# One written order of steps for each engine over all eight batches, in place of a loop over turns

## The chip, the cores and the metric

One core of a Trainium2 chip runs the kernel. The metric is device time in microseconds (us) from one launch. The engines named are PE (TensorE), DVE (VectorE), ACT (ScalarE), POOL (GpSimd) and SP (SyncE, which here only issues DMAs). Each engine takes its own instructions strictly in order, and engines meet at semaphores.

## The reference

Input x is 8 batches of 256 tokens by 128 features. Each batch passes four blocks, each closed by a residual sum and a LayerNorm:

```
x = layernorm(x + attention(x))   # 16 heads, a standard and a "geometric" softmax, both causal, mixed by a gate
x = layernorm(x + ffn(x))         # 128 -> 352 -> 128, activations and weights rounded to FP4 in blocks of 16
x = layernorm(x + mamba(x))       # 256 channels, 16 states, recurrence hc = a*hc + b over 256 tokens
x = layernorm(x + lora_ffn(x))    # 128 -> 512 -> 128, with a correction made from tokens 1 to 16
```

No batch depends on another.

## The kernel before

Every part of the work is a Python generator. A `yield` ends a step, and a step is a wait or two with the few instructions behind it. The parts, with the letters that the changed kernel uses for them:

- `prep` (p): transposes x, makes q, k, v and the line vectors, and splits them in three bf16 parts, which SP stores to DRAM and loads back as the attention's operands (L574, L588).
- `core` (c): 24 blocks of scores on PE with the row maximum on DVE (L1056). Then, with the maxima in the operands, 24 blocks again on PE, exponentials on ACT (L861) and the products with v on PE. ACT copies each half's sum out (att, L866).
- `norm_std` (N) and `norm` (n): divide by the softmax sums on DVE (L1078 to L1080: cstd, then cgeo), mix and project on PE, add the input (z, L1093), LayerNorm statistics (L974, L977), root on POOL (L732, L733), normalise on DVE (L985). N is one step; n has three on DVE: cgeo, z with its statistics, and the normalising that gives x1.
- `ffn` (f): 12 steps on DVE. The first five quantize x1 (L956 to L969), the rest is the gated product (L1110), its quantizing, z (L1101), and x2.
- `mamba` (m): hx (L1128), gate and convolution on PE, dbc (L1133), delta and u (L1137, L1141).
- `scan` (s), with `products` (u) on POOL (L769) and `rows` (r) on SP (L618): 16 DVE scans (L1152), each pair followed by the product with C (L1161, and L1157 for the last pair, half by half). PE sums the products in ps_y (9 steps). ACT makes the decay factors (L924), 16 steps.
- `mamba_out` (o): y (L1167), the projection into ps_n on PE, z (L1101) with statistics, x3.
- `lora_ffn` (l): the last block; y_out and its store.
- `warm` (w): matmuls of zeros into ps_y (two a step) which only keep PE active. There are 203 such steps in all with those of `warm_fill` and `warm_late`.
- `setup` (x): weights.

The kernel is pipelined over batches in **turns**. Turn k holds norm, ffn, mamba and scan of batch k, core and norm_std of batch k+1, prep of k+2, mamba_out and lora_ffn of k-1. `PLAN` gives, for each engine and part, a planned time for each step, and `interleave` issues the steps of a turn in the order of these times. All of a turn's steps are issued before any of the next. Turns -2 to 0 and 5 to 8 are written out; turns 1 to 4 are one body in a hardware loop, whose waits compare with register values. `EDGE` holds other times for turns -1, 0, 7 and 8.

```python
            for k in range(-2, 1):
                turn(k)
            with eng.Fori(1, BATCH - 3) as k:
                turn(k)
            for k in range(BATCH - 3, BATCH + 1):
                turn(k)
```

At the end of a steady turn the order on DVE is 25 steps s, then N. The next turn begins o n c c n o c c n o f f f f f. On PE the end is c s s s s N s, then n c p c n p n p c p c o. Written in letters, both repeat in each turn from 1 to 6 (turn 6 without the p).

Of the kernel before, what the change touches and what calls it, by code (L numbers as in the profile page):

```python
# [39 lines left out]
PLAN = {  # L40
    "sp": {
        "lora_ffn": [26.4, 57.5],
        "prep": [45.8, 57.7, 61.4, 63.8, 97.9, 101.2],
        "core": [48.9, 55.2, 55.3, 73.9, 76],
        "rows": [68.7, 71.2, 71.5, 71.8, 72.1, 82.9, 87.2, 90.1, 93.8],
    },
    "pool": {
        "core": [-2, 43],
        "prep": [15.5, 28.9, 40.6, 43.9],
        "lora_ffn": [31.2, 41.9],  # L50
        "mamba": [68.9],
        "products": [71.1, 72.4, 74.1, 75.4, 77, 78.3, 80.1, 81.4, 83.7, 85, 93.5, 94.8, 96.5, 97.8, 99.4, 99.6],
        "norm": [14.6],
        "ffn": [42.1, 42.2],
        "mamba_out": [15.8],
    },
    "act": {
        "prep": [10.4, 12.8, 14.9, 16.4, 17.9, 19.1, 22.9, 35, 42.3],
        "core": [0.3, 68.9, 69.5, 70, 70.5, 71, 72.6, 72.7, 77.4, 78.6, 79.2, 81.5, 82.6, 84.4, 84.9, 85.5, 85.6,
                 86.8, 87.4, 87.9, 90.5, 93.2, 93.3, 93.4, 93.8, 94.7, 96.6],  # L60
        "norm": [12.1],
        "lora_ffn": [21.7, 31.6],
        "ffn": [22.7, 28.8, 41.1],
        "mamba": [47.1, 47.2, 47.3, 47.6, 63.8, 65.3],
        "scan": [67.4, 69, 71.4, 75.5, 78, 79.3, 81.7, 82.9, 85.7, 86.5, 89, 92.4, 94.8, 94.9, 97.3, 98.5],
    },
    "dve": {
        "mamba_out": [2.8, 8.8, 13.9],
        "norm": [4.6, 7.8, 11.5],
        "core": [5.5, 6.1, 9, 9.6, 20.4, 21, 22.5, 24.3, 25.8, 34.1, 34.7, 36.7, 40.5, 45.6, 46.2, 47.4, 53.8, 55.5,  # L70
                 56.2, 56.9, 57.5, 58.7, 59.3, 59.9, 60.6, 62.6],
        "ffn": [15.8, 17.4, 17.8, 18.4, 19.4, 26, 28.8, 29.7, 30.8, 32.6, 38.5, 40.7],
        "prep": [22, 24.8],
        "lora_ffn": [23.9, 25.5, 36.2, 42.8],
        "mamba": [46, 55.1, 60.9, 77.7],
        "scan": [77.8, 77.9, 78, 78.1, 78.2, 78.3, 78.4, 78.5, 78.6, 78.7, 79.8, 81.1, 82.3, 83.5, 84.7, 87.7, 87.8,
                 92.1, 93.3, 94.5, 97.3, 98.7, 99.3, 99.9, 101.2],
        "norm_std": [110.4],
    },
    "pe": {  # L80
        "norm": [0, 2.4, 3.7],
        "prep": [0.9, 2.8, 3.9, 5, 6.6, 8.4, 24.1],
        "core": [0.8, 1.9, 4.1, 5.1, 7.3, 7.7, 17.7, 20.3, 21.5, 24.7, 25.2, 32, 35.5, 35.6, 37, 43, 49.7, 50.1, 51,
                 52.8, 53.4, 54.7, 55, 55.9, 56.6, 57.9, 58, 58.6, 60.1, 60.7, 61.6, 62, 63.3, 64.1, 64.4, 64.9,
                 65.5, 66, 66.7, 69.7, 70.4, 73.8, 74.2, 74.5, 75.1, 77.3, 77.7, 78, 78.7, 80.8, 81.2, 81.5, 82.4,
                 84.6, 84.9, 85.3, 85.6, 86.9],
        "mamba_out": [6],
        "lora_ffn": [13.5, 15.9, 21.6, 24, 26.1, 28],
        "ffn": [16.6, 19.2, 22.5, 22.6, 30.4, 32.8],
        "mamba": [42.2, 45, 45.1, 46, 50.8, 51.9, 52.1],  # L90
        "scan": [68, 71.6, 75.6, 86.2, 89.7, 97.5, 102.5, 105.9, 106.4],
        "norm_std": [106.1],
        "warm": [7.2, 7.6, 8.3, 13.1, 14.5, 21.1, 22.7, 38.3, 38.4, 39.5, 40.5, 41.5, 41.9, 42, 42.1, 42.5, 53.5,
                 57.8, 59.5, 61.5, 77.8],
    },
# [1495 lines left out]
```

## Time and profile before

| | us |
|---|---|
| median of 3 runs | 845.85 (844.6 to 849.32) |
| profiled execution, first to last instruction | 846.4 |
| PE busy | 706.0 (83%) |
| DVE busy | 610.1 (72%) |
| ACT busy | 409.4 (48%) |
| POOL busy | 396.6 (47%) |
| turns 1 to 6, from one y (L1167) to the next | 90.3 to 91.7 each |

The profile has no time of its own for the profiled execution besides its span; the span lies 0.55 us above the median of the runs, inside their spread. PE's busy time includes the matmuls of zeros.

### The profile page before, as it was taken

To read this page: it belongs to the slowest core of one execution; us is meant where nothing else is said; L and a number is where in the kernel's file an instruction comes from. 1 tells how busy PE (TensorE), PEld (TensorE's weight loads), DVE (VectorE), ACT (ScalarE), POOL (GpSimd) and SP (SyncE) were. 2 spreads that over 40 slices of the span, in tenths; PEclk is the share of its full clock that TensorE was granted. 3 is DMA by queue.
4 is the path that set the end of the run, shared out by engine and by line. 5 is a ranking of instruction groups with operands and counts; after the bars stand their busy time and mean duration, and the time that the engine had idled before them with its cause. 6 is when DMAs were issued, how large, how long until landed. Compare 5 with 4: busy or idle time off the path is not lost. (4 is left out here: it accounts for less than half of the span.)

```text
span 846.4 us, 12934 instructions
## 1 busy us (share of the span) xinstructions
PE 706.0 (83%) x4422; PEld 418.4 (49%) x4422; DVE 610.1 (72%) x1083; ACT 409.4 (48%) x832; POOL 396.6 (47%) x475
## 2 busy tenths in 40 slices
PE   5378768898889889997989888988898799876678
PEld 2244435445644565455645564456554564444235
DVE  1763475887869786969598677978697859744692
ACT  1225332763568254845385446815582438432532
POOL 6641322572449323952476344923393028411561
PEclk7679968999999999999999999999999999968898
DMA  5321200440035104420144013500442014000410
GB/s 132 85 97 61 98 25 21 153 160 9 26 129 168 51 0 133 130 107 0 53 166 147 5 39 127 173 27 1 152 131 85 1 34 158 26 0 7 146 55 7
DMA packets 41221, 66.12 MB, mean 78 GB/s; under 512 B 8041, under 2 KB 30398, under 8 KB 38846
## 3 DMA queue, kind: packets, MB, share of 16 engines
q1 hardware_dynamic: 39006, 64.58, 23.3%
q10 hardware_dynamic: 2176, 1.05, 0.4%
q8 instruction: 22, 0.36, 0.2%
q14 instruction: 17, 0.14, 0.1%
HBM read 57.68 MB, written 7.86 MB: 77 GB/s over the span
## 5 line engine op out<-in xcount | busy, mean ns | idle before, releaser
L769 POOL TENSOR_TENSOR shared<-u,bcrow 128x512 f32<-128x512 f32 x128 | 207.9, 1658 | 103.1 <-DVE u L1141 69.4
L1056 DVE TENSOR_REDUCE mx<-ps_s 128x2 f32<-128x512 f32 (+1 forms) x192 | 126.9, 685 | 68.3 <-PE ps_s L1195 66.4
L1195 PE MATMUL ps_s<-stack_mem 72*128 72x128 bf16 (+3 forms) x1024 | 138.9, 252 | 28.8 <-DVE mx L1056 16.8
L1152 DVE TENSOR_TENSOR_SCAN shared<-ps_f,shared 128x512 f32<-128x512 f32 x128 | 150.9, 1210 | 15.9 <-PE ps_y L1195 9.0
L1195 PE MATMUL ps_y<-shared,ident 128*128 128x512 f32 (+1 forms) x288 | 124.3, 566 | 12.3 <-DVE shared L1161 10.9
L924 ACT ACTIVATE ps_f<-delta,amat 128x255 f32<-128x255 f32 x256 | 110.2, 475 | 36.7 <-DVE shared L1152 22.6
L1195 PEld LDWEIGHTS ps_s<-stack_mem 74*128 74x128 bf16 (+1 forms) x1024 | 80.8, 100 | 90.3 <-DVE mx L1056 32.1
L1195 PE MATMUL ps_y<-zero_bf 128*128 128x512 bf16 x419 | 118.6, 396 | 1.2 <-DVE zero_bf L997 1.1
L861 ACT ACTIVATE probs<-ps_s 128x512 f32<-128x512 f32 x192 | 104.4, 596 | 20.0 <-PE ps_s L1195 20.0
L732 POOL TENSOR_TENSOR rstd<-mv,cst 128x2 f32<-128x2 f32 x32 | 6.2, 195 | 174.5 <-DVE mv L977 174.5
L1195 PEld LDWEIGHTS ps_y<-shared,ident 128*128 128x128 f32 x288 | 51.5, 193 | 58.7 <-issue 34.3
L1161 DVE TENSOR_TENSOR shared<-shared,bcrow 128x1024 f32<-128x1024 f32 x56 | 76.3, 1363 | 1.9
L1195 PE MATMUL ps_s<-causal,ident_bf 128*128 128x256 bf16 (+1 forms) x192 | 62.3, 326 | 4.1 <-DVE mx L1056 2.8
L1195 PEld LDWEIGHTS ps_y<-zero_bf 128*128 128x128 bf16 x419 | 41.8, 102 | 37.0 <-issue 12.9
L1195 PE MATMUL ps_s<-causalT,ident_bf 128*128 128x256 bf16 (+1 forms) x192 | 59.8, 312 | 0.2
L1195 PE MATMUL ps_v<-probs,vz 128*32 128x256 f32 (+1 forms) x1024 | 54.9, 332 | 4.1 <-ACT probs L861 3.8
L1195 PEld LDWEIGHTS ps_v<-probs,vz 128*32 128x32 f32 x1024 | 26.7, 109 | 41.4 <-ACT probs L861 20.5
L1195 PE MATMUL ps_n<-lmem 1*128 1x128 f32 (+1 forms) x224 | 32.3, 293 | 11.3 <-ACT lmem L935 6.5
L1195 PEld LDWEIGHTS ps_n<-lmem 1*128 1x128 f32 (+1 forms) x224 | 28.1, 198 | 20.2 <-ACT lmem L935 9.3
L715 POOL TENSOR_TENSOR vals<-vals,parts 128x1024 f32<-128x1024 f32 x8 | 17.7, 2216 | 39.8 <-ACT parts L844 39.8
L1195 PE MATMUL ps_f<-wguT,xqT_mem 128*128 128x352 f32 x64 | 33.0, 649 | 0.5 <-ACT xqT_mem L877 0.5
L790 ACT ACT_TABLE_LOAD x25 | 32.1, 1283 | 1.3 <-PEq L1576 0.8
(213 smaller groups left out, 1060.0 us busy)
## 6 DMA issues: line engine op xcount, KB each, us to landing
bcrow<-bc_dram SPq DMA_DIRECT2D x64, 512.0 KB, 4.2
stack_mem<-stack_dram SPq DMA_DIRECT2D x96, 192.0 KB
stack_dram<-parts SPq DMA_DIRECT2D x24, 256.0 KB, 2.3
x_tm<-in_L_attn_x_dram ACTq DMA_DIRECT2D x8, 128.0 KB, 2.1
xb<-in_L_attn_x_dram SPq DMA_DIRECT2D x8, 128.0 KB, 2.2
out_dram<-y_out SPq DMA_DIRECT2D x8, 128.0 KB, 2.0
fmem<-in_L_attn_conv_w_dram SPq DMA_DIRECT2D x1, 512.0 KB
...
```

The lines of the kernel that those rows point to most:

```text
L715: G.tensor_tensor(rest1[:], vals[:], parts[:, 0], ALU.subtract).then_inc(rest1_sb, 1)
L732: chain(G.tensor_tensor(dst, v, eps.to_broadcast([P, TT]), ALU.add))
L769: G.tensor_tensor(bx[:, j % 2, c], u[:, c].unsqueeze(1).to_broadcast([P, 2, T]), bcrow[:, j % RING, 0], ALU.mult).then_inc(bx_sb, 1)
L790: nc.scalar.preload_act_table_set("natural_log_exp_and_others")
L861: A(probs[:, g % 3, (n % 3) * 512:(n % 3 + 1) * 512], ps_s[:, n % 3], ACT.Exp).then_inc(p_exp, 1)
L924: last = A(adisc[:, c, n, 1:T], delta[:, c, 1:T], ACT.Exp, scale=amat[:, c, 2 * j + n:2 * j + n + 1])
L1056: V.tensor_reduce(mx[:, a, min(i, 1), hd[0]:hd[-1] + 1:2], ps_s[:, n % 2].rearrange("p (h n) -> p h n", h=len(hd)), AX.X, ALU.max).then_in ...
L1152: V.tensor_tensor_scan(hs[:, j % HB, c].rearrange("p n t -> p (n t)"), ps_f[:, c, :], bx[:, j % 2, c].rearrange("p n t -> p (n t)"), 0.0, ...
L1161: V.tensor_tensor(hs[:, j % HB], hs[:, j % HB], bcrow[:, j % RING, 1].unsqueeze(1).to_broadcast([P, NC, 2, T]), ALU.mult).then_inc(hc_dve, 1)
L1195: return nc.tensor.matmul(o, lhsT, rhs, start=start, stop=stop, **kw)
```

## The change

The tables `PLAN`, `EDGE` and `SPLIT`, the function `interleave`, the hardware loop and the clearing of the chain semaphores at each turn go. Each engine gets one string of letters for the whole run. Every letter issues the next step of its part, and a part goes to its next batch when its generator is through:

```diff
+class Stream:
+    def __init__(self, steps, batches=range(BATCH)):
+        self.steps, self.batches, self.now = steps, iter(batches), None
+
+    def step(self):
+        if self.now is None:
+            self.now = self.steps(next(self.batches))
+            next(self.now)
+        if next(self.now, DONE) is DONE:
+            self.now = None
...
+        def run(name, **streams):
+
+            streams = {letter: Stream(*s) if isinstance(s, tuple) else Stream(s) for letter, s in streams.items()}
+            for letter in "".join(ORDER[name].split()):
+                streams[letter].step()
...
             def ffn(b):
 
                 yield
+                if not is_first(b):
+                    dve.wait_ge(conv_ps, b * 2)
                 yield from quantize(flat(xq[:]), flat(x1[:]), T // BLK, T, xq_sb, xqT, flat(xq[:]))
...
+            def warm(_):
+                yield
+                if scanned[0] and not summing[0]:
+                    pe.wait_ge(yg_sb, scanned[0])
+                zero_step()
```

The number of steps of each letter is the same on every engine, the 203 warm steps among them. Only their order differs, and it now differs from turn to turn. From the strings, each turn's entry on DVE, beginning with N (s are the last scan steps of the batch before; before the change, all of them stood ahead of N):

```
turn 1:  N n o n c c o n f o c c f f f f
turn 2:  N s s s s n o n c c o n c c f o f f f f
turn 3:  N s s n o n o n f c c o f c f f f
turn 4:  N s n s s s s n o c c o n f f c o c f f f
turn 5:  N s l n s s n o n o f o c c f c c f f f
turn 6:  N s n s s n s s n f o f f f f
turn 7:  N s s s n s s n o n o f o f f f f
```

In turn 0, n n c c n f c f c f f f stands for c c c n c n n f f f f f. On PE, the first n of turns 2 to 7 stands ahead of the last one to three s, and in turns 4 to 6 its second and third too. From the entry of m on, DVE has m and 7 or 8 c, m and 5 or 6 c, then m m (before: m c c c m, 8 c, m c m). On PE c steps stand between the convolution steps of m (m c m c c m m c c m c c m c c m; before m w c m m m c c m c m m). Between PE's last m and last s stand 11, 11, 12, 8, 17 and 9 w in turns 1 to 6, where it was 5, and 34 c where it was 39 (31 in turn 4). Between the last f and the first m PE has 6, 1, 4, 3, 1 and 4 w where it was 8. On SP, in turns 4 and 5, the three stores of the parts (L574) stand behind the last r, not ahead of the first, and from turn 1 on one or both of the stack loads of `prep` (L588, six DMAs each) pass into the next turn, the second behind the load of x3's rows (l).

## Rows read from the trace of the kernel before

**Rows 1.** Windows by turn: length, busy PE PEld DVE ACT POOL, clock, DMA share, GB/s.

```profile
281.70:372.50 90.80, 80.80 (x541) 48.67 (x540) 72.59 (x131) 50.53 (x103) 47.80 (x56) 0.98 0.26 86
...
462.90:554.60 91.70, 82.06 (x540) 49.88 (x539) 72.67 (x131) 50.54 (x103) 47.79 (x56) 0.96 0.26 86
554.60:645.40 90.80, 80.92 (x541) 48.92 (x542) 72.62 (x132) 50.59 (x103) 47.79 (x56) 0.98 0.26 86
645.40:735.70 90.30, 78.86 (x519) 47.10 (x520) 71.94 (x126) 44.23 (x90) 33.81 (x30) 0.96 0.15 51
```

**Rows 2.** DVE in order of time, from turn 1 into 2: start, us, instruction, [idle before].

```profile
279.56 0.69 DVE L1157 TENSOR_TENSOR shared<-shared,bcrow 128x512 f32<-128x512 f32 x1
...
281.67 0.69 DVE L1167 TENSOR_TENSOR y<-ps_y,gsilu 128x512 f32<-128x512 f32 x1 [0.26 <-PE ps_y L1195]
...
282.89 0.42 DVE L1080 TENSOR_TENSOR cgeo<-ps_n,rec 128x256 f32<-128x256 f32 x1
283.23 1.28 DVE L1056 TENSOR_REDUCE mx<-ps_s 128x4 f32<-128x512 f32 x2
285.75 0.42 DVE L1093 TENSOR_TENSOR z<-ps_n,xb 128x256 f32<-128x256 f32 x1 [1.24 <-PE ps_n L1195]
...
286.73 0.25 DVE L977 BATCH_NORM_AGGREGATE mv<-bn 128x2 f32<-128x6 f32 x2
289.98 0.42 DVE L1101 TENSOR_TENSOR z<-ps_n,x2b 128x256 f32<-128x256 f32 x1 [3.01 <-issue]
...
292.54 0.60 DVE L985 TENSOR_SCALAR x<-z,mv,rstd 128x128 f32<-128x128 f32 x2
...
294.05 0.41 DVE L956 TENSOR_REDUCE qamax<-x 128x16 f32<-128x256 f32 x1
```

**Rows 3.** PE in order of time at the same place.

```profile
281.47 0.66 PE L1199 MATMUL ps_n<-ident,att 128*128 128x128 f32 x4
...
288.78 1.11 PE L1195 MATMUL ps_n<-moutw,y 128*128 128x128 f32 x8
```

**Rows 4.** ACT at the same place: the copy of the second half of attention.

```profile
273.75 0.60 ACT L866 ACTIVATE att<-ps_v 128x512 f32<-128x512 f32 x1 [0.44 <-PE ps_v L1195]
```

**Rows 5.** POOL at the same place: the second instruction of the root.

```profile
287.33 0.70 POOL L733 TENSOR_TENSOR rstd<-rstd,cst 128x2 f32<-128x2 f32 x1
```

**Rows 6.** DVE in turn 2, mamba and scan.

```profile
328.86 0.69 DVE L1056 TENSOR_REDUCE mx<-ps_s 128x4 f32<-128x512 f32 x1 [5.62 <-PE ps_s L1195]
...
330.56 0.47 DVE L1133 TENSOR_SCALAR dbc<-ps_f,dbcb 48x256 f32<-48x256 f32 x1
...
332.80 3.98 DVE L1056 TENSOR_REDUCE mx<-ps_s 128x4 f32<-128x512 f32 x6 [0.57 <-PE ps_s L1195]
336.70 0.42 DVE L1137 SCALAR_TENSOR_TENSOR delta<-fmem 128x256 f32<-128x256 f32 x1
...
339.73 1.22 DVE L1152 TENSOR_TENSOR_SCAN shared<-ps_f,shared 128x512 f32<-128x512 f32 x1
...
363.81 2.34 DVE L1152 TENSOR_TENSOR_SCAN shared<-ps_f,shared 128x512 f32<-128x512 f32 x2 [1.48 <-PE ps_y L1195]
```

**Rows 7.** Window from PE's last mamba step to its last scan step, turn 2.

```profile
332.20:372.30 40.10, 37.18 (x291) 19.11 (x290) 37.01 (x41) 29.45 (x69) 29.42 (x25) 1.00 0.47 164
```

**Rows 8.** The same window, matmuls of zeros alone (PE, PEld, DVE).

```profile
332.20:372.30 40.10, 2.96 (x10) 0.97 (x10) 0.00 (x0) 1.00 0.47 164
```

**Rows 9.** SP in order of time: the stack loads of turn 2.

```profile
355.87 10.22 SPq L588 DMA_DIRECT2D stack_mem<-stack_dram  x12
```

**Rows 10.** Instructions of the loop's line, by queue: ns min/median/max.

```profile
L524 PEldq COMPARE_BRANCH  x4: 76/210/239, 280.4 to 553.5; - x4
```

**Rows 11.** Turn 0: ACT's copy of attention.

```profile
90.28 0.60 ACT L866 ACTIVATE att<-ps_v 128x512 f32<-128x512 f32 x1 [0.98 <-PE ps_v L1195]
```

**Rows 12.** Turn 0: DVE's cgeo.

```profile
96.51 0.42 DVE L1080 TENSOR_TENSOR cgeo<-ps_n,rec 128x256 f32<-128x256 f32 x1
```

**Rows 13.** A window of the FFN's first matmuls in turn 2.

```profile
298.40:301.80 3.40, 3.40 (x11) 1.97 (x12) 2.37 (x5) 2.41 (x5) 0.00 (x0) 0.51 0.00 0
```

More of the change, by code:

```diff
@@ L37 @@
 LN_SHIFT = 20
[L40 to L95, printed above, removed]
-}
@@ L770, in products @@
                                         bcrow[:, j % RING, 0], ALU.mult).then_inc(bx_sb, 1)
-            def scan(b):
-                for j in POOL_HC:
-                    yield
-                    pool.wait_ge(hs_sb, b * 16 + 2 * j + 2)
-                    G.tensor_tensor(hs[:, j % HB], hs[:, j % HB], bcrow[:, j % RING, 1].unsqueeze(1).to_broadcast(S4),
-                                    ALU.mult).then_inc(hc_pool, 1)
-            run(pool, chain, "pool", ((prep, 2), (core, 1), (mamba, 0), (norm, 0), (ffn, 0), (products, 0), (scan, 0), (mamba_out, -1), (lora_ffn, -1)), setup)
+            run("pool", x=(setup, (0,)), p=prep, c=core, m=mamba, n=norm, f=ffn, u=products, o=mamba_out, l=lora_ffn)
         @block.scalar
@@ L937, in lora_ffn @@
                 exp_ln_tables()
-            run(act, chain, "act", ((prep, 2), (core, 1), (norm, 0), (ffn, 0), (mamba, 0), (scan, 0), (lora_ffn, -1)), setup)
+            run("act", x=(setup, (0,)), p=prep, c=core, n=norm, f=ffn, m=mamba, s=scan, l=lora_ffn)
         @block.vector
@@ L1186, in lora_ffn @@
                 (yield from layer_norm(2, b + 1, y_out, (y_stored, b * 16 + 16), b + 2)).then_inc(y_sb, 1)
-            run(dve, chain, "dve", ((prep, 2), (core, 1), (norm_std, 1), (norm, 0), (ffn, 0), (mamba, 0), (scan, 0),
-                                    (mamba_out, -1), (lora_ffn, -1)), setup)
+            run("dve", x=(setup, (0,)), p=prep, c=core, N=norm_std, n=norm, f=ffn, m=mamba, s=scan, o=mamba_out, l=lora_ffn)
         @block.tensor
@@ L1457, in mamba, with scan @@
                     mm(ps_f[:, c, 0:T], dupw[:, c * P:(c + 1) * P], dbc[:]).then_inc(dl_ps, 1)
[L1459 to L1461 removed]
+            def scan(b):
+                for j in range(N // 2):
                     halves = range(NC) if j == N // 2 - 1 else range(1)
@@ L1554, in lora_ffn @@
                 last.then_inc(f1_ps, 1)
-            run(pe, None, "pe", ((prep, 2), (core, 1), (norm_std, 1), (norm, 0), (ffn, 0), (mamba, 0), (scan, 0), (scan_late, -1), (warm, 0), (warm_fill, 1), (warm_late, -1),
-                                 (mamba_out, -1), (lora_ffn, -1)), setup)
+            run("pe", x=(setup, (0,)), p=prep, c=core, N=norm_std, n=norm, f=ffn, m=mamba, s=scan, w=(warm, range(10 ** 4)), o=mamba_out, l=lora_ffn)
 _INS = ['L0_attn_x', 'L0_attn_qkv_w', 'L0_attn_qkv_b', 'L0_attn_w1_write', 'L0_attn_w2_write', 'L0_attn_w1_read',
```

262 lines of the change are left out of this document (54 added, 208 removed), and 6 rows, old and new, of the table EDGE.

## The prediction

> **What bounds the kernel now.** I read the windows by turn first. Turns 1 to 6 take 90.3 to 91.7 us each. DVE works 72.6 us of turn 2 and PE 80.8, so no engine fills the turn [rows 1], and 11.3 of PE's 80.8 are matmuls of zeros (42 in that window). Then DVE in order of time, from one turn into the next [rows 2]. Here the reader is to see a chain with other work in its way. The last scan product ends at 279.56 + 0.69 = 280.25, and the quantizing of x1, with which the next batch's ffn begins, starts at 294.05: 13.8 us. In between are N, y, cgeo, two row maxima, z with statistics, a wait of 3.01 us for mamba_out's product, its z, two more maxima, x1 and x3. Attention's second half, all that x1 needs from outside, was copied out at 273.75 + 0.60 = 274.35 [rows 4], 5.9 us before the scan's end. It waited because every s stood ahead of n in the written order. So the period is the chain x1, ffn, mamba, scan, x1: 13.8 us of entry, then 45.7 from 294.05 to 339.7 and 31.4 of scan, 90.9 in all. The scan is DVE's own work but for one wait of 1.48 us for ps_y [rows 6]. Last the windows of PE: from its last mamba step to its last scan step it works 37.2 of 40.1 us [rows 7]. Ahead of that it has slack, inside it nearly none.
>
> **The change part by part.** Nothing is added to the arithmetic. I cost the order, by segments.
>
> Entry of the FFN. Prices [rows 2]: cgeo 1.03 (282.28 to 283.31), and N the same; from cgeo's end to its z 285.75 - 283.31 = 2.44 (PE mixes, ACT copies, PE projects); z with statistics 286.98 - 285.75 = 1.23, mamba_out's too; from statistics to a usable root about 1.1, since POOL is through at 288.03 [rows 5]; a pair of maxima 1.28; x1 and x3 0.60 each; y 0.69, not before 281.67 (1.4 after the scan's end); mamba_out on PE 1.11 plus about 0.3 to reach DVE [rows 3]. Laid end to end in the new order, counted from the scan's end, with what now stands inside the scan added:
> - Turn 1: cgeo to 3.0 (PE can turn att only behind its last scan step; in before it did so at 281.47 [rows 3]), y 3.7, z 5.4 to 6.7, maxima 8.0, mamba_out's z 8.1 to 9.3, x1 9.9. Saved 3.9. Moved in between the first two steps of quantizing: x3 and two maxima, 1.9. Net 2.0.
> - Turn 2: N in the scan (1.0); cgeo 1.0, y 2.1, z 4.0 to 5.2, maxima 6.5, mamba_out's z 7.8, x1 8.4, maxima 9.7. Saved 3.1, x3 inside costs 0.6. Net 2.5.
> - Turn 3: without the maxima 9.6. Saved 4.2; x3 and three maxima inside, 2.5. Net 1.7.
> - Turn 4: N and cgeo in the scan (2.1); z at once, maxima and y over PE's wait; x1 5.7. Saved 6.0, inside 1.9. Net 4.1.
> - Turn 5: cgeo before the last pair, whose 1.9 us cover most of the 2.44; x1 and mamba_out's z by 5.6. Saved 6.1, inside 3.2. Net 2.9. y_out's 0.6 is also put into this scan, but leaves the way of hx.
> - Turn 6: cgeo and z (3.3 with N, some 0.5 of wait) in the scan, x1 at once. Saved 9.4, y inside 0.7. Net 8.7.
> - Turn 7: as turn 5 (7.7). No core runs there, so I estimate the old entry at 13.8 less two pairs of maxima, 11.2. Saved 3.5, x3 inside 0.6. Net 2.9.
> Sum 24.8.
>
> Turn 0: att is there at 90.88 [rows 11], cgeo began at 95.90 and its main instruction at 96.51 [rows 12], behind maxima and PE's steps of prep. In the new order both n follow at once: 4.5 earlier, less two maxima inside the quantizing (1.3), and I take 3.5.
>
> What moved out of the entry (a pair of maxima, mamba_out's z, x3) needs cover. The waits of 5.62 and 0.57 between hx and delta [rows 6] are it, because PE now issues c between the convolutions. Price: two c on PE ahead of them, 1.2 us. Gain: between dbc and delta, six steps c instead of eight, of the 336.70 - 330.56 = 6.1 us between them, so 1.3 for two maxima, and mparts no longer between the deltas, some 0.5. I take 1.8. Net 0.6 a turn, 3.6 over six. If the cover is gone, 3 us a turn come back on the chain.
>
> Scan. PE's sums s2 and s3 now stand behind c49 to c53, not c44 and c56, so the 1.48 us wait should go: up to 9 us over six turns. But PE adds three n steps (2.2) and 3 to 12 w steps. At 2.96 us for 10 matmuls of which two are one step [rows 8], a step is 0.59 alone and 0.43 in a row, so six more on average are 2.8, and five c fewer save 2.6. That is 37.2 + 2.4 = 39.6 of 40.1 us: PE is full. Bounds 0 and 9; I take 0, since the row of PE's window is the nearer one. ACT has three exponentials ahead of the first decay factor and 6 to 9 ahead of the third; it works 29.5 of that window's 40.1 us, and I cost it at nothing beyond the 0.8 already in the 1.8.
>
> SP. In turns 4 and 5 the stack loads start some 4 us later than 355.87, behind the parts' stores, and the six of the first half take half of 10.22 us [rows 9], so they land near 366 where PE wants them at 372.8 or earlier by the gain: hidden. The second half now waits behind x3's rows, to about 14 us into the turn, and is wanted after 33: hidden. If the first weren't, PE's c, and y behind it, would be late by the excess. The wait on conv_ps in ffn is for a convolution of the batch before, 60 us old: nothing. The 203 w steps stay.
>
> Loop. Its branch takes 0.21 us on PE, four times [rows 10]. Turn 2 in the loop and turn 5 written out both take 90.80, turn 4 in the loop 91.70 [rows 1]: removing the loop is worth 0 to 1.5 us; I take 0. The Trainium skill (Runtime: NRT & Kernel Launch, Instruction fetch mechanics) says that a taken branch whose target lies outside the fetched window stalls for a DMA, and speaks for writing loops out. By it alone the change would gain something at each of four jumps; the equal turns say that this kernel hides it.
>
> Sum: 24.8 + 3.5 + 3.6 = 31.9. Seven entries are seven different orders, and with in-order engines each step that stands a little too early is paid in full, so I take three quarters: 23.9. **846.4 - 23.9 = 822.5 us.** The profiled span stands for the run; the median is 0.55 lower, which I leave in the range.
>
> **The rivals.**
> - The whole sum comes through and the ps_y waits go too, at two thirds of their 9: 846.4 - 31.9 - 6, about 808. For it: the longest waits of rows 2 and 6 all go. Against it: rows 7.
> - PE becomes the bound: the fills inside the scan window delay the sums, y follows PE, and only the slack ahead of m counts. The window then grows by the 2.4 us of work in six turns, 14 of the 24 are gone: about 837.
> - Slower: a wait on attention in front of the scan's sums. PE now has n ahead of s6 to s8, and DVE has cgeo ahead of the last scans. Att came 5.9 us before the scan's end; if it comes later than 3 us before that end, every further us holds both engines. It cancels the gain of 31.9 / 6 = 5.3 a turn when att slips by 2.9 + 5.3 = 8.2 us. ACT's new order, decay factors later, exponentials earlier, speaks against a slip. At 10 us slip, 6 x 1.8 above even: about 857.
> - The change does nothing: turns are held by something I don't see, and only the loop counts: 845 to 846.
> - The clock. One stretch in turn 2 ran at 0.51 of full, 1.2 GHz, in the FFN's first matmuls [rows 13], just behind a stretch in which PE waited for the quantizing. Fewer fills stand before m now. If each turn got one more such stretch on the chain, at half of 3.4 us, 7 x 1.7 = 12 us would be lost: 834. The Trainium skill (TensorE: Matmul & The Clock Gate, HAM oscillation) tells that waits of this kind bring the clock down; this row agrees.
>
> **How the numbers follow.** Chances: my forecast 0.55 (own range 812 to 832), whole sum 0.13, PE bound 0.12, clock 0.06, slower 0.07, nothing 0.07. A measurement here can tell 0.5%, that is 4.2 us. Faster by more (under 841.6): 0.86; within: 0.07; slower: 0.07. The range goes down to 803, which takes in the first rival, and up to 840, which takes in PE and clock and leaves out the last two.
>
> **What would show it.** In the profile after: y to y about 86 to 88 in turns 1 to 5 and the shortest into turn 6; from the last scan product to the quantizing 8 to 10 us in turns 1 to 3, about 5 in turns 4 and 5, under 2 in turn 6; the 3.0 us wait at mamba_out's z gone or under 1.5; cgeo between scans from turn 4 on; mx waits between hx and dbc down from 5.6; PE busy nearly as before in a shorter span. Wrong if cgeo waits for attention inside the scan, if DVE's wait for ps_y grows, if PE waits for the stack loads, or if the old waits show up again between f and m in equal size.

## The result and the profile after

| | before | after |
|---|---|---|
| median | 846.11 us (844.6 to 849.32) | 826.16 us (824.2 to 830.62) |
| ratio after / before | | 0.976, 95% interval 0.9725 to 0.9797 |
| profiled execution: time, span, granted clock | no time of its own, 846.4 span, 0.929 | 825.88, 824.1 span, 0.915 |

The change takes 20 us off, at a lower granted clock. Medians here and below are over all executions, while ratios leave out those over 1.5% above the same kernel's fastest (two of six in e6, one of six in e12). The page of the changed kernel, its first lines:

```profile
span 824.1 us, 12171 instructions
## 1 busy us (share of the span) xinstructions
PE 712.8 (86%) x4422; PEld 423.6 (51%) x4422; DVE 619.5 (75%) x1083; ACT 409.3 (50%) x832; POOL 394.3 (48%) x475
```

Windows from y to y, turns 1 to 6, columns as in [rows 1]:

```profile
185.50:272.20 86.70, 78.03 (x534) 47.76 (x535) 74.75 (x132) 50.35 (x103) 47.55 (x56) 1.00 0.31 105
272.20:365.40 93.20, 84.79 (x540) 51.46 (x540) 75.44 (x132) 51.06 (x103) 45.68 (x56) 0.93 0.21 73
365.40:459.80 94.40, 87.30 (x557) 53.85 (x557) 78.47 (x137) 51.12 (x106) 47.57 (x57) 0.91 0.27 86
459.80:546.10 86.30, 78.18 (x543) 48.19 (x542) 74.96 (x131) 50.54 (x103) 48.23 (x56) 1.00 0.28 90
546.10:633.50 87.40, 80.71 (x542) 49.30 (x540) 77.82 (x137) 49.81 (x102) 48.38 (x58) 0.98 0.29 89
633.50:720.00 86.50, 79.42 (x513) 47.77 (x513) 70.33 (x120) 44.23 (x90) 32.37 (x28) 0.92 0.20 67
```

Four turns lost 3.4 to 5.4 us against the 90.3 to 91.7 of before. Turns 2 and 3 got longer, and theirs is the clock that fell, to 0.93 and 0.91. Turn 6, which was to be the shortest, runs at 0.92 too.

DVE from turn 5 into turn 6, the place that answers to [rows 2]:

```profile
622.47 0.33 DVE L887 RECIPROCAL rec<-ps_n 128x32 f32<-128x32 f32 x1
...
625.75 0.42 DVE L889 TENSOR_TENSOR cgeo<-ps_n,rec 128x256 f32<-128x256 f32 x1
626.09 1.21 DVE L963 TENSOR_TENSOR_SCAN shared<-ps_f,shared 128x512 f32<-128x512 f32 x1
...
628.61 0.42 DVE L902 TENSOR_TENSOR z<-ps_n,xb 128x256 f32<-128x256 f32 x1 [0.58 <-PE ps_n L1005]
...
631.13 0.69 DVE L968 TENSOR_TENSOR shared<-shared,bcrow 128x512 f32<-128x512 f32 x1
631.74 0.60 DVE L794 TENSOR_SCALAR x<-z,mv,rstd 128x128 f32<-128x128 f32 x2
632.37 0.42 DVE L765 TENSOR_REDUCE qamax<-x 128x16 f32<-128x256 f32 x1
...
633.53 0.69 DVE L978 TENSOR_TENSOR y<-ps_y,gsilu 128x512 f32<-128x512 f32 x1
```

N, cgeo and z stand between the scan steps, x1 follows the last product (L968) at once, and y comes inside the quantizing: 0.5 us from scan end to qamax, against 11.6 into turn 6 before (13.8 into turn 2, [rows 2]). Into turn 3 it took 7.9 us:

```profile
363.32 0.81 DVE L968 TENSOR_TENSOR shared<-shared,bcrow 128x512 f32<-128x512 f32 x1
...
367.51 0.42 DVE L902 TENSOR_TENSOR z<-ps_n,xb 128x256 f32<-128x256 f32 x1 [1.47 <-PE ps_n L1005]
...
370.11 0.42 DVE L910 TENSOR_TENSOR z<-ps_n,x2b 128x256 f32<-128x256 f32 x1 [1.37 <-issue]
...
372.02 0.42 DVE L765 TENSOR_REDUCE qamax<-x 128x16 f32<-128x256 f32 x1
...
374.98 1.93 DVE L794 TENSOR_SCALAR x<-z,mv,rstd 128x128 f32<-128x128 f32 x2
```

The wait of 3.01 us at mamba_out's z [rows 2] is 1.37. But x3's normalising, moved into the quantizing, takes 1.93 us for its two instructions, where [rows 2] has 0.60.

**Where the time went.** The chain cut at its milestones on DVE, from the two traces (us; turns 1 to 7 summed):

| segment | before | after | difference |
|---|---|---|---|
| up to batch 0's qamax of x1 | 103.1 | 108.1 | +5.0 |
| from there to batch 0's scan end | 87.0 | 74.6 | -12.4 |
| entries: scan end to qamax of x1 | 92.1 | 43.3 | -48.8 |
| qamax to quantized x1 | 22.6 | 41.7 | +19.1 |
| quantized x1 to gated hidden (hff) | 56.2 | 62.6 | +6.4 |
| hff to z of the FFN | 81.6 | 81.5 | -0.1 |
| z to first scan | 162.4 | 159.5 | -2.9 |
| scan, with what was put in | 217.9 | 229.8 | +11.9 |
| last scan end to the end | 23.5 | 23.0 | -0.5 |

Each segment runs from the start of one instruction to the start of the next one named, scan end apart. qamax is the first instruction of the quantizing of x1, hff the gated product. Together -22.3, which is 824.1 - 846.4. (For z to first scan the two middle parts, to hx and on, are added.)

### The profile page after: what moved, and what is told of

Its sections match the earlier page's. It is cut to its first block and busy times, and to the rows that moved or that the text cites. A ratio compares the mean times of both kernels' runs of the same rounds, so it can differ in the third digit from the quotient of the medians.

```text
span 824.1 us, 12171 instructions
## 1 busy us (share of the span) xinstructions
PE 712.8 (86%) x4422; PEld 423.6 (51%) x4422; DVE 619.5 (75%) x1083; ACT 409.3 (50%) x832; POOL 394.3 (48%) x475
## 5 line engine op out<-in xcount | busy, mean ns | idle before, releaser
L586 POOL TENSOR_TENSOR shared<-u,bcrow 128x512 f32<-128x512 f32 x128 | 203.6, 1620 | 64.1 <-DMA bcrow<-bc_dram 34.3
L963 DVE TENSOR_TENSOR_SCAN shared<-ps_f,shared 128x512 f32<-128x512 f32 x128 | 151.1, 1208 | 11.8 <-ACT ps_f L733 7.1
L1005 PE MATMUL ps_s<-stack_mem 72*128 72x128 bf16 (+3 forms) x1024 | 143.7, 260 | 7.7 <-DVE mx L865 5.6
L1005 PE MATMUL ps_y<-shared,ident 128*128 128x512 f32 (+1 forms) x288 | 121.8, 553 | 8.8 <-DVE shared L972 8.0
L1005 PEld LDWEIGHTS ps_s<-stack_mem 74*128 74x128 bf16 (+1 forms) x1024 | 83.8, 102 | 63.0 <-DVE mx L865 19.4
L972 DVE TENSOR_TENSOR shared<-shared,bcrow 128x1024 f32<-128x1024 f32 x56 | 78.9, 1409 | 1.8
L1005 PE MATMUL ps_s<-causalT,ident_bf 128*128 128x256 bf16 (+1 forms) x192 | 61.5, 323 | 2.1 <-DVE mparts L872 2.1
L1005 PE MATMUL ps_v<-probs,vz 128*32 128x256 f32 (+1 forms) x1024 | 56.2, 338 | 1.8 <-ACT probs L670 1.4
L1005 PEld LDWEIGHTS ps_v<-probs,vz 128*32 128x32 f32 x1024 | 27.1, 110 | 33.4 <-ACT probs L670 13.8
L1005 PE MATMUL ps_n<-lmem 1*128 1x128 f32 (+1 forms) x224 | 37.7, 326 | 5.5 <-ACT lmem L744 3.0
L1005 PEld LDWEIGHTS ps_n<-lmem 1*128 1x128 f32 (+1 forms) x224 | 33.3, 228 | 14.9 <-ACT lmem L744 5.3
L1005 PE MATMUL ps_f<-wguT,xqT_mem 128*128 128x352 f32 x64 | 30.5, 611 | 3.9 <-ACT xqT_mem L686 2.4
```

The costliest lines, as they stand in the source:

```text
L586: G.tensor_tensor(bx[:, j % 2, c], u[:, c].unsqueeze(1).to_broadcast([P, 2, T]), bcrow[:, j % RING, 0], ALU.mult).then_inc(bx_sb, 1)
L963: V.tensor_tensor_scan(hs[:, j % HB, c].rearrange("p n t -> p (n t)"), ps_f[:, c, :], bx[:, j % 2, c].rearrange("p n t -> p (n t)"), 0.0, ...
L972: V.tensor_tensor(hs[:, j % HB], hs[:, j % HB], bcrow[:, j % RING, 1].unsqueeze(1).to_broadcast([P, NC, 2, T]), ALU.mult).then_inc(hc_dve, 1)
L1005: return nc.tensor.matmul(o, lhsT, rhs, start=start, stop=stop, **kw)
```

## The experiments

Steps are written with letter, batch and number: s1.24 is step 24 of batch 1's scan, w a step of zeros. All kernels are the changed one with another order, and compute the same; e3, e6, e7, e8, e9 and those built on them also have another number of steps of zeros. A minus in a diff is the changed kernel's order where nothing else is said. The changed kernel itself had 826.16, ratio 0.976.

**e1_old_order.** The former order on every engine, written out without the loop.

```diff
-    "dve": "ppxpxxxxxxxxcccc..."      # the new order
+    "dve": the letters of the former turns -2 to 8, one turn after another
```

> The old kernel's order of steps, turn by turn, written out as one string per engine in the new code: no hardware loop, no register values in the waits, no clearing of semaphores. If the loop is worth nothing (my costing, 0 to 1.5 us), 845 to 846 us and turns of 90.3 to 91.7 us. If the loop itself cost time (fetch stalls at the jumps), turns 1 to 4 get shorter and turns 5 and 6 don't, and the time falls towards 826.

Measured: 845.46 median (841.16 to 853.26), ratio 1.001 (0.9963 to 1.0054). The loop and its branch are worth nothing here, to within the 4 us of the interval; the 20 us are in the order.

**e2_setup.** One DVE step of batch 1's preparation, which waits 10.65 us in the middle of the weights' set-up, behind it.

```diff
- dve: x0.0 p1.0 x0.1 ... x0.8 c0.0 c0.1
+ dve: x0.0 x0.1 ... x0.8 c0.0 p1.0 c0.1
```

> The changed kernel with one DVE step moved: the first prep step of batch 1 (line squares' sums) goes behind the nine setup steps and the first maximum, where it was in the old order. In the changed kernel DVE waits 10.65 us at that step for POOL, in the midst of quantizing the weights, and the first row maximum starts at 56.2 us, not 50.6. If that in-order wait is what made the start late: first maximum near 51, time 820 to 822. Rival: the start is late from PE's low clock in the first core (27.3 us at 1.2 GHz from 57.7), and the moved step gives back under 1 us.

Measured: 827.76 (826.97 to 832.93), ratio 0.9799 (0.9723 to 0.9876); the first maximum at 56.9. The wait only moved: DVE was done sooner, and then waited 9.28 us for ACT's copy of the weights. ACT and PE had their own steps still in the new places; e6, which puts them back on every engine, has the first maximum at 49.7. So the late start is not this one step's.

**e3_fills_core0.** Nine steps of zeros more on PE inside batch 0's core, where the former order had them.

```diff
- pe: c0.2 c0.3 ... c0.10 c0.11 ... c0.56 c0.57
+ pe: c0.2 w c0.3 ... c0.10 w c0.11 ... c0.56 w c0.57
```

> The changed kernel with nine more steps of matmuls of zeros in the first batch's core on PE, behind the same core steps as in the old kernel. From the first row maximum to the copy of attention's second half it took 39.7 us before (clock 0.97) and 43.4 in the changed kernel (27.3 us at 1.2 GHz). If missing fills brought the clock down there: 40 us and clock near 1.0 in that stretch, time 821 to 823, all else being equal. Rival: the clock is low for the waits on DVE's setup just ahead; then the stretch stays at 43 and the time at 826 or a little above.

Measured: 827.88 (826.59 to 831.56), ratio 0.9794 (0.972 to 0.9868). From first maximum to last att copy it takes 43.6 us with them and 43.4 without, although the granted clock there rose from 0.69 to 0.77. That is the rival: the fills were not what batch 0 lacked.

**e5_entry_undone.** On DVE and PE every step n of batches 1 to 7 back behind the last scan step of the batch before; all else new.

```diff
- dve: s5.19 N6.0 s5.20 n6.0 s5.21 s5.22 n6.1 s5.23 s5.24 n6.2 f6.0 o5.0
+ dve: s5.19 N6.0 s5.20 s5.21 s5.22 s5.23 s5.24 n6.0 n6.1 n6.2 f6.0 o5.0
- pe: s5.5 n6.0 w w w n6.1 w n6.2 s5.6 s5.7 w s5.8 c7.0
+ pe: s5.5 w w w w s5.6 s5.7 w s5.8 n6.0 n6.1 n6.2 c7.0
```

> The changed kernel with the passing of the turn boundary by norm undone: on DVE and PE every n of batches 1 to 7 stands behind the last scan step of the batch before; all other steps keep their order. By the entries measured in the changed kernel (with cgeo and z taken out of the scan and laid behind it): turn 4 about +3, turn 5 +2, turn 6 +4, turn 7 +2, so 834 to 838 us. If passing the boundary is the whole gain, 846. If it is worth nothing because PE bounds the scan, 826.

Measured: 846.27 (840.95 to 852.45), ratio 1.001 (0.997 to 1.0052). That is the 846 named for "the whole gain", not the 834 to 838 worked out from the entries. DVE into turn 6, from the profiled execution, which at 852.45 was the slowest of ten:

```profile
647.82 0.69 DVE L968 TENSOR_TENSOR shared<-shared,bcrow 128x512 f32<-128x512 f32 x1
650.72 0.36 DVE L887 RECIPROCAL rec<-ps_n 128x32 f32<-128x32 f32 x1 [2.21 <-PE ps_n L1009]
...
654.20 0.42 DVE L902 TENSOR_TENSOR z<-ps_n,xb 128x256 f32<-128x256 f32 x1 [2.44 <-PE ps_n L1005]
...
656.58 0.60 DVE L794 TENSOR_SCALAR x<-z,mv,rstd 128x128 f32<-128x128 f32 x2 [1.16 <-POOL rstd L552]
```

8.7 us of entry with three waits, which the former order filled with maxima and y, and y is 9.9 us late here. Without the passing of the boundary nothing of the change's gain is left. But this isn't the former kernel again. Its entries add up to 71.1 us, still 21 less than before, and the 19.1 us more between qamax and quantized x1 eat most of that. Against the changed kernel the entries are 27.8 longer and the scans 7.6 shorter: the passing is worth 20 us net in this order. It doesn't follow that the passing alone would do, and the next run says it doesn't.

**e7_entry_on_old_order.** The former order, with turn 6's entry at each boundary into turns 2 to 7 and the other steps moved only as far as that needs, ACT's too (the minus is the former order; three steps of zeros fewer).

```diff
- dve: s3.24 N4.0 o3.0 n4.0 c5.0 c5.1 n4.1 o3.1 c5.2 c5.3 n4.2 o3.2 f4.0
+ dve: s3.19 N4.0 s3.20 n4.0 s3.21 s3.22 n4.1 s3.23 s3.24 n4.2 f4.0 o3.0 f4.1 ... f4.4 c5.0 c5.1 o3.1 c5.2 c5.3 o3.2
- pe: s3.7 N4.0 s3.8 n4.0 c5.0 p6.0 c5.1 n4.1
+ pe: N4.0 s3.4 s3.5 n4.0 s3.6 n4.1 n4.2 s3.7 s3.8 p6.0 c5.0 o3.0
```

> The former order on every engine, with one thing changed at the six boundaries into turns 2 to 7: on DVE the division of att, cgeo, z and the normalising of x1 stand between the last scan steps and the quantizing's maximum of x1 right behind the last scan step, ahead of y; x3's steps go between the scores' maxima behind the quantizing; PE's att transposes and the attention's output projection stand ahead of its last two scan steps; ACT's combT copy right behind its last decay; each engine's batch b+3 preparation and the LoRA steps move only as far as these need. Theory E (the entry alone carries the gain, and can be had at each boundary): from scan end to the maximum of x1 0.5 to 2 us in place of 13.8 in turns 2 to 7, the scan 3 to 4 longer for the steps put in, 1 to 3 more inside the quantizing; net 6 to 8 each, 36 to 48 in all: 798 to 812. Rival F (att comes too late for it: in the old order its last copy stands 6.1 to 6.6 us ahead of the scan's end, and cgeo then holds up the last scan steps by 1 to 3 us a turn; the preparation of b+3, pushed back, delays the next scores' maxima by 2 to 4): net 2 to 4 each, 822 to 834. Rival G (the other reorderings of the change are what makes room): 840 or more.

Measured: 881.85 (875.41 to 883.53), ratio 1.041 (1.0357 to 1.0455): on the side of rival G (840 or more), but 36 us slower than before, which no theory had. The entries are 0.5 to 0.6 us at every one of the six boundaries, 75 us less than before over turns 1 to 7. The segment behind them, quantized x1 to hff, grew from 6.6 to 8.3 (10.0 in turn 7) to between 14.9 and 25.8. So late attention (rival F) is not what costs: cgeo waits for it 0.75 us a turn. Something of the FFN's middle is late.

**e8_entry6_in_4_5_7.** The same entry, in the changed kernel, for turns 4, 5 and 7; PE and ACT follow (not shown), with three steps of zeros more.

```diff
- dve: s3.19 N4.0 s3.20 n4.0 s3.21 ... s3.24 n4.1 o3.0 c5.0 c5.1 o3.1 n4.2 f4.0 f4.1 c5.2 o3.2 c5.3
+ dve: s3.19 N4.0 s3.20 n4.0 s3.21 s3.22 n4.1 s3.23 s3.24 n4.2 f4.0 o3.0 f4.1 ... f4.4 c5.0 c5.1 o3.1 c5.2 c5.3 o3.2
```

> The new kernel with turn 6's way into the FFN given to turns 4, 5 and 7 too, whose way now takes 5.1 to 5.3 us against 0.5 in turn 6. Theory E: 3 to 4.5 less on each entry, less about 1 us that y or x3's steps then cost inside the quantizing and its gaps: net 2 to 3.5 each, 815 to 820. Rival B (PE or ACT has become the bound of these turns, 84 to 86 us of work in a turn of 86 to 87): y to y stays at 86 to 87, within 2 us of 826. Rival H (x3 and the LoRA steps come late and hold up the LoRA stage and POOL's root behind them, which the next turn waits for): 828 or more.

Measured: 838.55 (835.18 to 845.54), ratio 0.992 (0.988 to 0.9957): 12 slower than the change. Rival H. PE in turn 4:

```profile
474.58 1.35 PE L1005 MATMUL ps_f<-wguT,xqT_mem 128*128 128x352 f32 x4
...
480.27 1.15 PE L1005 MATMUL ps_n<-lmem 1*128 1x128 f32 x8
...
483.30 2.02 PE L1005 MATMUL ps_n<-lmem 1*128 1x128 f32 x8 [1.44 <-DVE lmem L989]
485.25 2.71 PE L1005 MATMUL ps_f<-wguT,xqT_mem 128*128 128x352 f32 x4
```

The FFN's gate matmuls are through at 475.9, its up matmuls start at 485.25: they stand behind both LoRA products of the batch before, and the second of these waits for w1e, the first LoRA weight sum, on DVE (L989), which needs the first product, which needs x3. x3 now comes after the quantizing. The entry was won and the LoRA chain, in the same queues, took it back: 19.6 us from quantized x1 to hff in turn 4.

**e11_hff_first_6_7.** In turns 6 and 7 hff on DVE ahead of the two LoRA sums.

```diff
- dve: c7.5 l5.0 l5.1 f6.5 f6.6
+ dve: c7.5 f6.5 l5.0 f6.6 l5.1
- pe: l6.2 f7.2 f7.3
+ pe: f7.2 f7.3 l6.2
```

In the changed kernel, turn 6:

```profile
643.83 0.75 DVE L989 SCALAR_TENSOR_TENSOR lmem<-ps_n,lscale,w1T 128x512 f32<-128x512 f32 x1 [1.87 <-PE ps_n L1005]
646.63 0.75 DVE L992 SCALAR_TENSOR_TENSOR lmem<-ps_n,lscale,w2T 128x512 f32<-128x512 f32 x1 [2.05 <-PE ps_n L1005]
647.30 0.88 DVE L921 TENSOR_TENSOR fmem<-fmem,ps_f 128x704 f32<-128x704 f32 x1
```

> The new kernel with the gate-times-up product (hff) of turns 6 and 7 ahead of the two LoRA weight sums (w1e, w2e) on DVE, and in turn 7 the up matmuls ahead of the second LoRA product on PE. Theory L (in turn 6 x1 enters 8 us earlier, but hff then stands behind w1e and w2e, which wait for x3's late chain: the product could start at about 642.5 and started at 647.3): quantized x1 to hff in turn 6 falls from 11.1 to 6 to 7, turn 7's by 0 to 3: 819 to 823. Rival C (hff is late for the lower clock of those microseconds alone): turn 6 stays at 10 to 11, 825 to 827. Rival M (the LoRA steps then come late for ACT's hqT copy or the mamba part behind them): what is gained at hff is lost between quantized hidden and z1, within 1.5 of 826.

Measured: 830.31 (828.06 to 832.99), ratio 0.981 (0.9769 to 0.9854). Turn 6: quantized x1 to hff 6.4 us, as expected of theory L. But the hidden's quantizing took 9.4 for 6.6 with the sums in it, and from there to z 10.9 for 6.5. ACT:

```profile
655.00 0.84 ACT L744 ACTIVATE lmem<-ps_n,b1c 128x256 f32<-128x256 f32 x2 [7.68 <-PE ps_n L1005]
659.90 0.84 ACT L744 ACTIVATE lmem<-ps_n,b1c 128x256 f32<-128x256 f32 x2 [4.06 <-PE ps_n L1005]
660.75 1.28 ACT L599 ACT_TABLE_LOAD   x1
663.86 0.60 ACT L694 ACTIVATE fmem<-ps_f 128x512 f32<-128x512 f32 x1 [1.83 <-PE ps_f L1009]
```

The hidden was quantized at 656.6; its copy (L694) started at 663.86, behind both LoRA gelus. That is rival M, and more than a stand-off, for the median is 4 us over the changed kernel's, though the intervals of the two ratios overlap: the LoRA chain is in the way at whichever of the two places it meets the FFN.

**e13_entry6_mended.** e8's entries with the up matmuls and hff ahead of the LoRA steps, on top of the prologue, fills and hff edit of e12 (below). The minus is e8's order.

```diff
- pe: c5.4 p6.5 w l3.1 c5.5 l3.2 f4.2 f4.3 l3.3
+ pe: f4.2 f4.3 c5.4 p6.5 l3.1 c5.5 w l3.2 l3.3
- dve: c5.4 c5.5 l3.0 l3.1 p6.1 f4.5 f4.6
+ dve: c5.4 f4.5 l3.0 c5.5 f4.6 l3.1 f4.7 p6.1
```

> As e12_all_three, and turns 4, 5 and 7 get turn 6's way into the FFN as in e8_entry6_in_4_5_7, but with the up matmuls on PE and hff on DVE ahead of the LoRA products and sums. Theory L (what e8_entry6_in_4_5_7 lost was hff behind the LoRA steps: 18 to 20 us from quantized x1 to hff in turns 4 and 5): quantized x1 to hff 7 to 10 in turns 4 and 5, so 1 to 4 less than e12_all_three a turn, or 3 to 9 in all: 802 to 809. Rival Q (preparation of b+3, pushed behind the entry, and the former batch's steps that the scores wait for take the time anyway): turns 4 and 5 no shorter than in e12_all_three, equal to 5 above it.

Measured: 840.42 (837.98 to 848.63), ratio 0.995 (0.9919 to 0.9982), 21 slower than e12 and far outside both expectations. In turns 4 and 5 quantized x1 to hff fell to 13.7 and 12.3, still above e12's 6.6 and 5.8, and hff to z rose from 11.0 and 12.0 to 19.2 and 17.6. Theory L, as put, falls: hff was one of the meetings, not the only one.

**e14_lora_behind_ffn.** The former prologue and e9's fills, and in turn 6 the LoRA chain put behind the FFN on all engines.

```diff
- act: f6.0 f6.1 l5.0 l5.1 f6.2
+ act: f6.0 f6.1 l5.0 f6.2 l5.1
- pe: f6.2 f6.3 l5.1 l5.2 l5.3 c7.6 w w w w l5.4 w l5.5 c7.7 f6.4 c7.8 c7.9 f6.5
+ pe: f6.2 f6.3 l5.1 c7.6 w w w w l5.2 w c7.7 f6.4 l5.3 c7.8 c7.9 f6.5 c7.10 c7.11 w w l5.4 c7.12 c7.13 w w l5.5
```

> The new kernel with the former prologue and the fills of e9_fills_at_waits (not the edit of e11_hff_first_6_7), and in turn 6 the whole LoRA chain of batch 5 interleaved behind the FFN on all engines: w1e on DVE behind the hidden's first quantizing product, w2e behind the quantized hidden, the LoRA sum behind hx; ACT's hqT copy ahead of the LoRA gelus; PE's second LoRA product and its hidden behind hff's matmuls and around the transposes of the quantized hidden; POOL's root for it behind the FFN's. Additive part: 826.2 less 6.9 less 5.8 is 813.5, with turn 6 as in e9_fills_at_waits (11.4 from quantized x1 to hff, 6.1 from quantized hidden to z1). Theory L (the LoRA chain of the batch before, in the same queues and started no earlier than x3, is what turn 6 gave its entry's gain back to): 6 to 7, 7 to 8 for the quantizing with the two inserted parts, and 4.5 to 5: 3 to 5 less in turn 6, 808 to 811. Rival S (the LoRA chain, put off, holds up something later as the scores' maxima or the mamba part): turn 6's z1 to y grows by as much, 812 to 817.

Measured: 818.54 (814.64 to 824.05), ratio 0.970 (0.9644 to 0.9753). In turn 6, against e9's trace: to hff 7.7 for 11.4, quantizing 7.3 for 6.6, to z 6.3 for 6.1, but hx to dbc 13.1 for 11.7 and the scan with turn 7's entry 42.1 for 39.6. The 3.7 us won at hff are lost again by the next qamax, as rival S has it; the median lies 1.5 us above S's range. Which wait the LoRA chain causes there was not traced further. No order run here keeps the gain.

**e6_prologue_old.** The steps ahead of turn 0 in the former order, with that order's fills (five more on PE).

```diff
- pe: p1.0 p1.1 p1.2 w x0.0 x0.1 p1.3 w w p1.4 p1.5 c0.0 w w x0.2 c0.1
+ pe: p1.0 x0.0 x0.1 p1.1 x0.2 p1.2 p1.3 p1.4 c0.0 p1.5 c0.1
- act: p1.0 p1.1 p1.2 x0.0 c0.0 x0.1 p1.3 p1.4 x0.2
+ act: p1.0 x0.0 x0.1 p1.1 c0.0 p1.2 x0.2 p1.3 p1.4
```

> The steps ahead of turn 0 (all of batch 0's preparation and attention, part of batch 1's preparation, with their fills on PE) go in the former order on every engine; all that follows keeps the new one. Theory P (the prologue of the new order costs time that the whole run pays): the first maximum comes at about 51 us in place of 56.2, the last att copy of batch 0 at 90 to 94 in place of 99.6, batch 0's y comes 5 to 9 us earlier than 185.5, and so does the end: 817 to 821. Rival A (absorbed: the FFN of batch 0 then waits for something else of turn 0, as batch 1's core, and y of batch 0 stays within 2 us of 185.5): 824 to 827.

Measured: 819.3 (813.66 to 828.75), ratio 0.965 (0.9596 to 0.9701), the one interval that lies below that of the change. The first maximum on DVE, and ACT's last att copy of batch 0, after the change:

```profile
56.20 1.98 DVE L865 TENSOR_REDUCE mx<-ps_s 128x4 f32<-128x512 f32 x3 [2.46 <-ACT wdT L617]
```

```profile
99.57 0.60 ACT L675 ACTIVATE att<-ps_v 128x512 f32<-128x512 f32 x1 [0.98 <-PE ps_v L1005]
```

and in e6:

```profile
49.72 0.69 DVE L865 TENSOR_REDUCE mx<-ps_s 128x4 f32<-128x512 f32 x1 [3.72 <-PE ps_s L1005]
```

```profile
91.53 0.60 ACT L675 ACTIVATE att<-ps_v 128x512 f32<-128x512 f32 x1 [0.98 <-PE ps_v L1005]
```

In e6 y of batch 0 comes at 177.3, after the change at 185.5, before at 191.3. Theory P holds: the new prologue costs about 8 us up to there, and the 12.4 gained behind it are turn 0's own, since e6 keeps them (73.3 us from qamax to scan end).

The span of this trace is only 4.5 us shorter than the changed kernel's. 3.8 of the 8.2 are gone by turn 1, where quantized x1 to hff took 9.4 us at a low clock, not 5.7. From qamax to hff:

```profile
184.20:200.40 16.20, 12.85 (x48) 8.10 (x47) 10.98 (x26) 7.45 (x13) 7.78 (x17) 0.77 0.21 75
```

The changed kernel has 1.00 there, and so do e12 and e14 (5.7 us each), whose order up to that place is e6's. So this fall belongs to the execution, not to the order.

**e9_fills_at_waits.** 25 steps of zeros more at waits of PE in turns 2, 3, 6 and 7.

```diff
- pe: p5.3 w c4.2 c4.3 l2.0
+ pe: p5.3 w w w w w w w c4.2 c4.3 l2.0 w w w
```

> The new kernel with 25 more zero steps on PE at waits of 1 to 2 us just ahead of stretches at the lower clock (turns 2, 3, 6 and 7: ahead of the LoRA steps and, in turn 3, ahead of the third score step; in turn 7 also ahead of mamba's output projection). Theory C (those waits are what takes the clock there, and the low clock's matmuls in the FFN cost what they take longer): the stretches of 10.2 at 286, 17.1 at 375 and 17.1 at 727 shrink or go, quantized x1 to gated hidden in turns 3 and 6 to 7 falls from 11 to 12 to 6 to 7 us: 4 to 5 each in three turns, 812 to 816. Rival K (the clock falls there from what PE did over longer, the waits filled or not): within 1 us of 826, or slower by the fills that stand ahead of awaited matmuls, 827 to 830.

Measured: 820.33 (817.18 to 823.49), ratio 0.970 (0.9664 to 0.9745), between theory C's 812 to 816 and rival K's 825 or more. The interval overlaps that of the change; all six executions lie under the change's four. Windows of turn 3 in the changed kernel:

```profile
371.70:375.10 3.40, 1.67 (x9) 0.71 (x7) 3.11 (x9) 0.84 (x2) 3.32 (x6) 1.00 0.01 2
375.10:378.50 3.40, 2.57 (x10) 1.57 (x11) 3.33 (x6) 0.00 (x0) 1.64 (x2) 0.51 0.01 2
378.50:382.00 3.50, 3.50 (x14) 2.41 (x11) 2.53 (x6) 0.67 (x2) 0.00 (x0) 0.50 0.38 131
382.00:385.40 3.40, 2.93 (x8) 1.55 (x8) 1.35 (x2) 2.38 (x5) 0.00 (x0) 0.50 0.51 190
385.40:388.80 3.40, 3.40 (x14) 2.27 (x12) 1.47 (x5) 3.15 (x5) 0.27 (x2) 0.50 0.06 22
```

and at the same work in e9:

```profile
367.00:370.40 3.40, 3.40 (x17) 1.79 (x18) 3.11 (x8) 0.84 (x2) 3.29 (x6) 1.00 0.01 2
370.40:373.80 3.40, 2.66 (x18) 1.53 (x17) 3.33 (x7) 0.00 (x0) 1.82 (x2) 1.00 0.01 2
373.80:377.20 3.40, 3.24 (x19) 2.14 (x17) 2.94 (x8) 0.67 (x2) 0.00 (x0) 1.00 0.45 125
377.20:380.60 3.40, 2.93 (x17) 1.93 (x15) 2.09 (x5) 3.16 (x7) 0.00 (x0) 1.00 0.48 178
```

PE worked 1.67 us of the window ahead of the fall, and then 17.1 us ran at half clock (1.2 GHz), the FFN's four gate matmuls in 2.71 us. With the wait filled the clock stays at 1.00 (2.4 GHz) and they take 1.45. Quantized x1 to hff: turn 2 from 11.1 to 7.2, turn 3 from 12.1 to 7.2, turn 7 from 10.2 to 5.9, turn 6 not (11.1 and 11.4: that one is the LoRA sums, as e11 shows). The other traces bear this out. Turn 2 takes 7.2 us in all four kernels that have these fills, and 9.6 to 11.2 in the seven others with the new order there. Turn 3 takes 7.2 in the four and 11.4 to 12.1 in six of the seven; in e2 it took 7.1 without a fill. So the wait makes the fall likely, not certain. Theory C holds for three turns of four. Of the 11.8 us that these stretches lose over turns 1 to 7, 8.7 reach the span: among other things the entry into turn 7, where four of the fills stand ahead of the awaited product of mamba_out, went from 5.3 to 7.5. The Trainium skill (TensorE: Matmul & The Clock Gate, HAM oscillation) says that waits between groups of matmuls bring the lower clock again and again; its waits are for DMA, these for DVE, and these runs agree.

**e12_all_three.** The prologue of e6, the fills of e9 and the edit of e11.

```diff
+ the diffs of e6_prologue_old, e9_fills_at_waits and e11_hff_first_6_7, together
```

> The former prologue, the fills at the waits of turns 2, 3, 6 and 7, and hff first in turns 6 and 7, together. If the three are separate costs they add up: 6.9 for the prologue, 5.8 for the fills, 3 to 5 for hff: 809 to 813. If the prologue's and the fills' gains are the same microseconds of clock, or hff's is in the fills' already: 814 to 819.

Measured: 819.41 (814.07 to 826.78), ratio 0.971 (0.9658 to 0.9758), above both expected ranges. Since the hff edit by itself costs 4.2, additive medians would give 826.2 - 6.9 - 5.8 + 4.2 = 817.7: within 2 us. By the ratios, where e6 is 0.0113 and e9 0.0057 under the change and e11 0.0050 over it, they would give 0.964, 6 us less than measured. And e14, without that edit, should by the medians have come to 813.5 and came to 818.5. By profiled spans e6 is 4.5 and e9 8.7 under the change's 824.1, and e12 11.8. No kernel here is shown to be faster than e6 or e9. Whether the prologue's and the fills' gains add up fully stays open: the executions of e12 and e14 lie 12.7 and 9.4 us apart.

## Why the prediction was right, and what in it was not

822.5 was forecast as a span; 824.1 was measured, and 826.16 as the median. The cause forecast, the entry past the turn boundary, is the cause shown: the entries took 48.8 us less, and e5, which takes the passing back, loses the gain. That the sum came so near is in part luck. Its 31.9 undiscounted met 36.6 - 19.1 + 7.4 + 2.9 + 0.3 - 6.4 + 0.1 + 0.5 = 22.3 (entries net of what was put into the scans, quantizing, start and turn 0, z to first scan, scan, quantized x1 to hff, hff to z, the end). Point by point:

- **Entries.** Forecast from scan end: 9.9, 9.7, 8.6, 5.7, 5.6, 0.6, 5.6. Measured: 9.7, 9.7, 7.9, 5.1, 5.1, 0.5, 5.3. Saved, less N, cgeo, z and y_out put into the scans (12.2 by my prices): 36.2 forecast, 48.8 - 12.2 = 36.6 measured. Inside it two errors cancel: turn 6's old entry was 11.6, not the 13.8 I took, and turns 3, 4 and 7 saved more.
- **Work moved inside the quantizing.** This term was mis-sized most: 11.4 forecast, 19.1 measured. Most of the difference is not queueing. Beside POOL's line products x3's two instructions took 1.2 to 2.0 us in turns 1 to 5, not 0.60: 5.0 too much in all, and the small qscale and qinv another 2.
- **Turn 0.** The step "att is there at 90.88 ... I take 3.5" failed. From att's copy to qamax 8.6 us replaced 12.8, 4.2 less for the 3.5 I took, but att came 9.3 later, because I costed nothing of the reordered prologue (+5.0 at qamax; 8 by e6). And the new order of turn 0 behind it gained 12.4, of which I had seen nothing: hff came 5.5 after quantized x1 where it was 10.1, hidden's quantizing 6.6 for 8.9, hx to dbc 11.4 for 13.3, the scan 30.0 for 32.4. Two blind spots of opposite sign, net 7.4 for 3.5.
- **Mamba.** 3.6 forecast, 2.9 measured (z to first scan). dbc to delta went from 6.1 to 5.3, and the longest wait of a maximum from the 5.62 of [rows 6] to 3.3 (first line below). Right in sum, but both parts came at about half: hx to dbc is 3.5 longer over turns 1 to 7, where I priced two c at 1.2 a turn (7.2), and dbc to the first scan 5.7 shorter, where I took 1.8 a turn (10.8).
- **Scan.** 0 forecast, 0.3 measured: 11.9 longer for 12.2 put in. Right in sum and wrong in both parts. The waits for ps_y (1.48 in [rows 6], 9.0 us in all) went completely, so the row of PE's window was the wrong one of my two bounds. But DVE now waits more for ACT's decay factors, 7.1 us for 2.3, which I had costed at nothing; 4.6 of it are in scans 5 and 6. For the transposes of att it waits next to nothing in the scans: of L887's 21.1 us, 19.8 lie in the start and turn 0, 0.8 in turn 1's entry, and 0.2 and 0.3 at the cgeo of turns 5 and 6. Scans 1 to 4 gained 3.0 net of what was put in, 5 and 6 lost 2.5. The waits of DVE in the changed kernel (us in all, times, longest):

```profile
DVE mx L865 <- PE ps_s L1005: 34.3, 44, 3.3
DVE rec L887 <- PE ps_n L1009: 21.1, 5, 16.2
...
DVE shared L963 <- ACT ps_f L733: 7.1, 7, 3.3
```

- **Clock.** It was a rival at 0.06, for up to 12 us, and in no term of the sum. It took part: quantized x1 to hff is 2.8 longer in turn 2 and 5.5 in turn 3 (over turns 1 to 7 it is 6.4, with turn 6's 2.9 for the LoRA sums and 4.8 less in the four others), and e9 gives 5.8 back by filling waits. The place, fewer fills ahead of the FFN's matmuls, is the one I named.
- **Loop.** 0, and e1 has 0, to within 4 us. The Trainium skill's rule (Runtime: NRT & Kernel Launch, Instruction fetch mechanics), that jumps out of the fetched window stall, would have given a gain; e1 shows none.
- **SP.** The stack loads were forecast hidden, and PE waits for none of them in the trace after.
- **PE bound.** e9 puts 25 steps more on PE and gets faster. So PE's queue isn't full in the turns' boundaries. In the scan window it stayed untested.
- **The discount.** I took three quarters of 31.9 for steps that stand too early. 22.3 came, 0.70. The reason was the wrong one, in part: the loss lay in slowed instructions, the prologue and the clock, and a flat quarter happened to cover them.
- **The signs.** Entries, the 3.0 us wait (1.37), cgeo between scans and PE busy (712.8 for 706.0) came as forecast. Of the turns, 2 and 3 did not: 93.2 and 94.4 for 86 to 88. Nor was turn 6 the shortest: it took 86.5, turn 4 86.3. Of the signs of being wrong, cgeo's wait inside the scan showed up, with 0.3 us at most, and waits between f and m did grow: DVE waits 13.1 us for the second LoRA product (L992) and 8.8 for the up matmuls (L921), for 7.3 and 5.5 before.
- **What I didn't forecast at all** is that turn 6's entry can't be had elsewhere. Its 0.5 us looked free. e7, e8, e11 and e13 show its price: x3 comes later, and all of the LoRA chain with it, into the FFN's queues. In turn 6 itself hff waits for it, 11.1 us for 8.2.
